# A mixture-of-experts tail in 140 units: row buffers for 32 units, landings reported five units late, a longer table of needs, blank units without weight loads

## The chip, the cores and the metric

The kernel runs on one NeuronCore of a Trainium2 chip. The time is the device time of one execution in microseconds (us). The kernel before took 716.58 us, the median of three runs (715.09 to 717.36). The engines are TensorE (PE, matmuls), VectorE (DVE), ScalarE (ACT), GpSimd (POOL, which issues the indirect DMAs here) and SyncE (SP, which issues nearly all other DMAs). Each runs its own list of instructions in order; they meet at semaphores. A DMA adds 16 to a semaphore when its data has landed.

## The reference

```
x = x + gnn(layernorm(x))          # 128 x 128 x 128 floats: 16384 tokens of 128
xf = layernorm(x).reshape(-1, 128)
top_w, top_i = top_k(xf @ Wg + bg, 2);  top_w = softmax(top_w)
for e in range(8):                 # H = 512
    h = gelu(xf @ W1[e] + b1[e])
    out = out + w_dense[:, e:e+1] * (h @ W2[e] + b2[e])
x = x + out
```

The biases bg of this input are uneven, so that the experts get very different numbers of tokens: of the lower-numbered of a token's two experts 2866, 2285, 657, 3756, 328, 6492, 0, 0 tokens fall on experts 0 to 7, and of the higher-numbered one 0, 33, 6, 172, 8, 297, 15868, 0. (These are counts of the reference's own choices for this input.)

## The kernel before

**Two stages.** The first takes the tokens in 16 chunks: the graph layer, the second layernorm, the two experts of each token, and its place in a list sorted by expert. POOL scatters the rows (260 floats: the normalised token, the running sum, weights, and where to go next) into `rows` in HBM, expert by expert. The second stage takes sorted rows in **units** of 256 rows of one expert. There are two passes, the first over the lower-numbered experts of all tokens, the second over the higher-numbered ones, with 70 units each (`NU`), so units 0 to 69 and 70 to 139. The first 32 units (`NE`) are full units that can start before all chunks are counted.

**What a unit does.** SP loads its 256 rows (`rows_in`, line 504, 260 KB), its expert's biases (`biases_in`, 532), and, only if the expert differs from that of three units before, each layer's weights (`layer_in`, 520, 512 KB a layer, into one of three slots). PE transposes the rows (1606), does layer 1 (1620 to 1622, 12 matmuls), layer 2 of the unit before (1633, 1634, 1638, 12 matmuls), and turns back the outputs of the unit two before (1649). ACT applies gelu, and DVE splits the values into high and low parts (1420, 1426). `sum_up` on DVE (1435, 1440) adds the expert's output to the rows of the unit three before; it stands ahead of the split of the current unit. POOL then scatters the 256 rows with two indirect DMAs (`scatter`): to their place for the second pass (line 691), or in the second pass to the output (688).

**SP's order.** At step k SP issues: layer 1's weights and the biases of unit k+2, layer 2's weights of unit k+1, then the rows of unit k+6. Each waits in that one list: weights for a free slot (the matmuls of three units before), rows for two things. One is the **buffer**: rows live in a ring of 16 buffers (`GR`), so that unit t waits until the scatter of unit t-16 has landed; units 0 to 31 use `first_rows`, space left by the first stage, and units from 32 on use `got`, so that units 32 to 47 find theirs free. The other is for units of the second pass the **need**: the number of first-pass units whose scattered rows must have landed. It is looked up in a table on the chip for the first 12 of them (`EARLY`); the 13th waits for all. The table is read into SP's registers by `entries` (line 486), 16 steps at a time.

**Reports.** POOL counts landings for SP in `s_landed` (line 674): before it hands over the scatter of unit t, its list waits until unit t-3 has landed, adds one, then waits for `sum_up` of unit t. The semaphore starts at 1.

**The experts here.** From the counts above and the code follow, before and after alike: units 0 to 31 hold experts 0, 1, 2, 3 and 5; units 32 to 37 expert 0, 38 to 41 expert 1, 42 and 43 expert 2, 44 to 49 expert 3, 50 and 51 expert 4, 52 to 66 expert 5, 67 to 69 are blank (nothing to do, same weights). In the second pass 70 and 71 are blank, 72 to 75 hold experts 1, 2, 3, 4, 76 and 77 expert 5, 78 to 139 expert 6. Weights are loaded in the kernel before for units 38 to 40, 42 to 46, 50 to 54 and 70 to 80 (among others). Unit 78 and all after it need 67 landed units, 0 to 66.

Of the kernel before, what the change touches and what calls it, by code (L numbers as in the profile page):

```python
# [8 lines left out]
I32 = mybir.dt.int32  # L9
U32 = mybir.dt.uint32  # L10
ALU = mybir.AluOpType
# [3 lines left out]
P = 128  # L15
# [70 lines left out]
def program(nc, x, x_turned, adj, edges, gate_weights, gate_biases, Wg, bg, W1, W2, biases, out):  # L86
# [15 lines left out]

    EARLY = 3 * GR // 4

# [6 lines left out]
    FULL = CHUNKS - 6  # L111
    NE = 2 * GR

    RING = 5
# [7 lines left out]

    ALL = 48 * (UNITS // 48 + 1)

    def unit(k):
# [15 lines left out]
    with ExitStack() as ctx:  # L141
        def sb(name, shape, dt=F32):
            return ctx.enter_context(nc.sbuf_tensor(name, list(shape), dt))

        def sem(name):
            return ctx.enter_context(nc.semaphore(name))
# [116 lines left out]
        got = row[:, 1:5].rearrange("p r (s j) k -> p (r s) j k", j=BLK)  # L263
        got_i = got.bitcast(I32)

# [8 lines left out]
        def rows_of_unit(t):  # L274
            return first_rows[t.slot(GR)] if t.index < NE else got[:, t.slot(GR)]
        to_row = sb("to_row", [P, GR, BLK], I32)
        in_hi = sb("in_hi", [P, IN, TILE], F32R)
# [122 lines left out]
        s_done = sem("unit_summed")  # L400
        s_out = [sem(f"unit_rows_scattered{i}") for i in range(GR)]

# [6 lines left out]
        def _(sp):  # L409
# [88 lines left out]
            def rows_in(t, both):  # L498
                if t.real:
                    at = sp.snap(both >> 4, min_val=0, max_val=BLANK + 1)  # L500
                    g = t.slot(GR)
                    if not NE <= t.index < NE + GR:
                        wait_slot(sp, s_out, 16 * BLK, t, 0)
                    sp.dma_start(rows_of_unit(t).rearrange("p j k -> p (j k)"),
                                 rows[bass.ds(at, TILE)].rearrange("(p j) k -> p (j k)", j=BLK)).then_inc(s_got[g], 16)
# [79 lines left out]
            for first in range(NE, UNITS, UT):  # L585
# [5 lines left out]
                for k in range(first, min(first + UT, UNITS)):  # L591
# [6 lines left out]
                    if k + AHEAD < UNITS:  # L598
                        wait_landed(k + AHEAD, needs)
                        rows_in(unit(k + AHEAD), early[k + AHEAD - NU] if 0 <= k + AHEAD - NU < AHEAD else now[i])  # L600
            for i in range(GR):
                sp.wait_ge(s_out[i], 16 * BLK * ((UNITS + GR - 1 - i) // GR))

        @block.gpsimd
        def _(pool):
# [66 lines left out]
            def landed(t):  # L672
                wait_slot(pool, s_out, 16 * BLK, t, 16 * BLK)
                pool.sem_inc(s_landed, 1)

            def scatter(t):
                second = t.index >= NU
                if 0 <= t.index - 3 < NU:
                    landed(t.back(3))
                wait_turn(pool, s_done, 1, t, 1)  # L680
                g = t.slot(GR)
                for j in range(BLK):
                    if t.index < NE:
                        at = bass.IndirectOffsetOnAxis(ap=rows_of_unit(t).bitcast(I32)[:, j, NEXT_AT:NEXT_AT + 1], axis=0)
                    else:
                        at = bass.IndirectOffsetOnAxis(ap=to_row[:, g, j:j + 1], axis=0)
                    if second:
                        pool.indirect_dma_start(out=out_rows, out_offset=at, in_=got[:, g, j, P:2 * P], in_offset=None,  # L688
                                                bounds_check=TOKENS - 1, oob_is_err=False).then_inc(s_out[g], 16)
                    else:  # L690
                        pool.indirect_dma_start(out=rows, out_offset=at, in_=rows_of_unit(t)[:, j, :], in_offset=None,  # L691
                                                bounds_check=NROWS - 1, oob_is_err=False).then_inc(s_out[g], 16)
# [179 lines left out]
        def _(dve):  # L872
# [7 lines left out]
            dve.memset(node_least[:, 0:2], 0.0).then_inc(s_iota, 1)  # L880
            dve.tensor_scalar(node_least[:, 2:3], node_i[:], -float(WR), 0.0, ALU.add, ALU.min).then_inc(s_iota, 1)
            dve.tensor_copy(slot_f[:], slot_i[:]).then_inc(s_iota, 1)
# [407 lines left out]
            def units_begun():  # L1290
# [11 lines left out]

                own(dve.tensor_tensor(change[:], expert[:, 2], expert[:, 0], ALU.not_equal))
                own(dve.tensor_reduce(first, at_unit[:, 0], AX_X, ALU.add))
# [123 lines left out]
            def sum_up(t):  # L1428
                g, second = t.slot(GR), int(t.index >= NU)
                held = rows_of_unit(t)  # L1430
                at = TOKEN_AT if second else NEXT_AT

                if t.index >= NE:
                    i = t.index if second else t.index - NE
                    dve.scalar_tensor_tensor(out=to_row[:, g, :], in0=skip[:, i, :], scalar=BIG, in1=got_i[:, g, :, at],
                                             op0=ALU.mult, op1=ALU.max)
                wait_turn(dve, s_o, 1, t, 1)
                for j in range(BLK):
                    w = held[:, j, W_AT + second:W_AT + second + 1]
                    last = dve.scalar_tensor_tensor(out=held[:, j, P:2 * P], in0=ps_o(t)[:, j, :], scalar=w,  # L1440
                                                    in1=held[:, j, P:2 * P], op0=ALU.mult, op1=ALU.add)
                last.then_inc(s_done, 1)
# [277 lines left out]
```

## Time and profile before

| what | value |
|---|---|
| median of three runs | 716.58 us (715.09 to 717.36) |
| the profiled execution | 716.63 us, its span 714.9 us |
| PE, ACT, DVE, POOL busy | 91%, 83%, 81%, 70% of the span |
| second stage | from about 214 us to the end |

The span is the time from the first to the last instruction of the profiled execution; 1.7 us lie around it. A profile view "waits" says who waited for whom; a timeline row is an instruction with its start, its length and, in brackets, the idle time of its engine before it and what ended it. Busy times of PE overlap within a stream, so stalls are read best from starts.

### The profile page before, as it was taken

To read this page: it belongs to the slowest core of one execution; us is meant where nothing else is said; L and a number is where in the kernel's file an instruction comes from. 1 tells how busy PE (TensorE), PEld (TensorE's weight loads), DVE (VectorE), ACT (ScalarE), POOL (GpSimd) and SP (SyncE) were. 2 spreads that over 40 slices of the span, in tenths; PEclk is the share of its full clock that TensorE was granted. 3 is DMA by queue.
4 is the path that set the end of the run, shared out by engine and by line. 5 is a ranking of instruction groups with operands and counts; after the bars stand their busy time and mean duration, and the time that the engine had idled before them with its cause. 6 is when DMAs were issued, how large, how long until landed. Compare 5 with 4: busy or idle time off the path is not lost.

```text
span 714.9 us, 18241 instructions
## 1 busy us (share of the span) xinstructions
PE 647.8 (91%) x4879; PEld 589.7 (82%) x4879; DVE 578.9 (81%) x2041; ACT 596.1 (83%) x1613; POOL 498.2 (70%) x471
## 2 busy tenths in 40 slices
PE   5979898998849999999998999998999999999991
PEld 4546665666539999899997999988999999999991
DVE  5899999999987889987876778776778787878781
ACT  4789999999968978788886878876888888888881
POOL 2643767666765677788777778777677777677774
PEclk9999999899979999999999999999999999999997
DMA  8999995548246897959999985689754444444211
GB/s 288 360 369 268 355 344 177 183 163 325 97 151 187 287 343 237 318 165 301 330 372 322 367 254 171 178 329 359 233 153 126 124 127 122 129 121 129 73 42 34
DMA packets 85500, 161.09 MB, mean 225 GB/s; under 512 B 32631, under 2 KB 36736, under 8 KB 85392
## 3 DMA queue, kind: packets, MB, share of 16 engines
q1 hardware_dynamic: 66032, 112.96, 50.4%
q0 software_dynamic: 18496, 46.70, 17.8%
q8 instruction: 41, 0.67, 0.4%
q14 instruction: 67, 0.55, 0.2%
q10 hardware_dynamic: 864, 0.21, 0.1%
HBM read 104.95 MB, written 57.23 MB: 227 GB/s over the span
## 4 chain that ended last, share of the span: by engine, by line
PE 31%; ACT 23%; POOL 14%; issue 12%; DVE 9%; DMA 7%; SPq 2%; POOLq 0%; DVEq 0%; ACTq 0%
POOL out_dram L688 8%; POOL rows L691 6%; ACT hs L750 5%; ACT row L759 5%; DMA rows<-row,to_row 4%; PE bank L1633 4%; PE bank L1638 4%; PE bank L1620 4%; PE bank L1634 4%; ACT t_loop L741 4%; PE bank L1621 4%; PE bank L1622 4%; ACT t_in L734 3%; PE bank L1606 2%; PE bank L1649 2%
## 5 line engine op out<-in xcount | busy, mean ns | idle before, releaser
L846 ACT ACTIVATE act_f<-bank,b_t 128x256 f32<-128x256 f32 x560 | 219.4, 476 | 23.3 <-PE bank L1622 13.0
L688 POOL DMA_INDIRECT out_dram<-row,to_row x140 | 164.0, 1171 | 60.9 <-issue 55.4
L1426 DVE TENSOR_TENSOR act_lo<-act_f,act_hi 128x1024 fp32r<-128x1024 f32 x140 | 172.0, 1229 | 12.1 <-ACT act_hi L850 0.2
L646 POOL DMA_INDIRECT rows<-row,slot_low x128 | 134.8, 1053 | 64.7 <-issue 34.1
L1420 DVE CAST act_hi<-act_f 128x512 fp32r<-128x512 f32 x140 | 61.5, 439 | 90.5 <-ACT act_f L846 90.4
L1620 PE MATMUL bank<-in_hi,w_t 128*128 128x256 f32 x376 | 113.8, 303 | 7.0 <-DMA w_t<-w_split 5.9
L691 POOL DMA_INDIRECT rows<-row,to_row x76 | 93.3, 1228 | 25.0 <-issue 20.9
L1622 PE MATMUL bank<-in_hi,w_t 128*128 128x256 f32 x376 | 105.7, 281 | 0.0
L1621 PE MATMUL bank<-in_lo,w_t 128*128 128x256 f32 x376 | 105.7, 281 | 0.0
L836 ACT ACTIVATE in_hi<-bank 128x256 fp32r<-128x256 f32 x140 | 53.9, 385 | 58.0 <-PE bank L1606 57.4
L1633 PE MATMUL bank<-act_hi,w_t 128*128 128x256 f32 x376 | 100.4, 301 | 0.0
L1634 PE MATMUL bank<-act_hi,w_t 128*128 128x256 f32 x376 | 92.2, 280 | 0.0
L850 ACT ACTIVATE act_hi<-act_f 128x512 fp32r<-128x512 f32 x140 | 90.8, 649 | 0.0
L1620 PEld LDWEIGHTS bank<-in_hi,w_t 128*128 128x128 f32 x376 | 71.4, 190 | 8.9 <-DMA w_t<-w_split 7.5
L1621 PEld LDWEIGHTS bank<-in_lo,w_t 128*128 128x128 f32 x376 | 71.6, 190 | 0.0
L1622 PEld LDWEIGHTS bank<-in_hi,w_t 128*128 128x128 f32 x376 | 71.2, 189 | 0.0
L1634 PEld LDWEIGHTS bank<-act_hi,w_t 128*128 128x128 f32 x376 | 70.9, 189 | 0.0
L1633 PEld LDWEIGHTS bank<-act_hi,w_t 128*128 128x128 f32 x376 | 70.8, 188 | 0.1
L856 ACT ACTIVATE y_t<-bank,b_t 128x256 f32<-128x256 f32 x140 | 65.6, 469 | 2.4 <-PE bank L1638 2.4
L1440 DVE SCALAR_TENSOR_TENSOR row<-bank,row 128x128 f32<-128x128 f32 x216 | 65.2, 344 | 1.6 <-PE bank L1649 1.6
L750 ACT ACTIVATE hs<-xs,shift,rstd 128x128 f32<-128x128 f32 x128 | 53.5, 645 | 8.6 <-DVE t_sum L990 6.6
L1414 DVE TENSOR_TENSOR in_lo<-bank,in_hi 128x256 fp32r<-128x256 f32 x140 | 58.1, 415 | 2.6 <-ACT in_hi L836 2.6
(278 smaller groups left out, 1787.6 us busy)
## 6 DMA issues: line engine op xcount, KB each, us to landing
row<-rows SPq DMA_DIRECT2D x108, 260.0 KB, 3.1
w_t<-w_split SPq DMA_DIRECT2D x52, 512.0 KB
w_up<-w_split SPq DMA_DIRECT2D x28, 512.0 KB
xs<-in_x_dram SPq DMA_DIRECT2D x16, 512.0 KB, 5.3
x_t<-in_x_turned_dram SPq DMA_DIRECT2D x16, 512.0 KB, 6.4
rows<-ends_rep SPq DMA_DIRECT2D x15, 260.0 KB, 7.7
xs<-rows SPq DMA_DIRECT2D x10, 260.0 KB
b_t<-in_biases_dram SPq DMA_DIRECT2D x140, 2.5 KB
```

The source lines that it names most:

```text
L646: pool.indirect_dma_start(out=rows, out_offset=bass.IndirectOffsetOnAxis(ap=slot_low[:, r, b:b + 1], axis=0), in_=row[:, r, b, :], in_offs ...
L688: pool.indirect_dma_start(out=out_rows, out_offset=at, in_=got[:, g, j, P:2 * P], in_offset=None, bounds_check=TOKENS - 1, oob_is_err=Fals ...
L691: pool.indirect_dma_start(out=rows, out_offset=at, in_=rows_of_unit(t)[:, j, :], in_offset=None, bounds_check=NROWS - 1, oob_is_err=False) ...
L750: last = act.activation(hs[:, t.slot(2), b, :], xs[:, t.slot(4), b, :], ACT.Identity, scale=rstd[:, 0, b:b + 1], bias=shift[:, 0, b:b + 1])
L846: last = act.activation(act_f[:, s, c, :], ps_h(t, half)[:, i, :], ACT.Gelu, bias=b_t[:, w, c:c + 1])
L850: act.activation(act_hi[:, t.slot(LATE + 1), 0:FC // 2], act_f[:, s, 0:FC // 2], ACT.Copy).then_inc(s_half, 1)
L1426: dve.tensor_tensor(act_lo[:, s], act_f[:, t.slot(2)], act_hi[:, s].bitcast(F32), ALU.subtract).then_inc(s_hlo, 1)
L1620: pe.matmul(dst, hi, in_hi[:, s], start=True, stop=False)
L1621: pe.matmul(dst, hi, in_lo[:, s], start=False, stop=False)
L1622: last = pe.matmul(dst, lo, in_hi[:, s], start=False, stop=True)
L1633: pe.matmul(ps_y(t), hi, act_hi[:, s, c, :], start=(c == 0), stop=False)
L1634: pe.matmul(ps_y(t), lo, act_hi[:, s, c, :], start=False, stop=False)
```

## The change

Four things. The ring gets 32 buffers (`LANES`): from unit 32 on a unit uses first the 16 of `got`, then the 16 of `first_rows`, and so on, and waits for the scatter of its buffer's last user (`lane`, `uses`); units 16 to 31 wait as before. POOL reports unit t-5, not t-3, before the scatter of unit t. Needs are looked up for 24 units. In the second pass a blank unit counts as one whose expert has not changed, so that it loads no weights, and the three units behind the blank ones do (here 70 and 71 load nothing; 72 to 80 load as before).

```diff
-    EARLY = 3 * GR // 4
+    EARLY = 24
...
+    LANES = 2 * GR
...
+    def lane(k):
+
+        return k % GR if k < NE else (GR + k - NE) % LANES
+
+    def uses(k):
+
+        return sum(lane(i) == lane(k) for i in range(k))
...
         def rows_of_unit(t):
-            return first_rows[t.slot(GR)] if t.index < NE else got[:, t.slot(GR)]
-        to_row = sb("to_row", [P, GR, BLK], I32)
+            i = lane(t.index)
+            return first_rows[i] if i < GR else got[:, i - GR]
+        to_row = sb("to_row", [P, LANES, BLK], I32)
...
-                    if not NE <= t.index < NE + GR:
-                        wait_slot(sp, s_out, 16 * BLK, t, 0)
+                    if uses(t.index):
+                        sp.wait_ge(s_out[lane(t.index)], 16 * BLK * uses(t.index))
...
             def landed(t):
-                wait_slot(pool, s_out, 16 * BLK, t, 16 * BLK)
+                pool.wait_ge(s_out[lane(t.index)], 16 * BLK * (uses(t.index) + 1))
                 pool.sem_inc(s_landed, 1)
 
             def scatter(t):
                 second = t.index >= NU
-                if 0 <= t.index - 3 < NU:
-                    landed(t.back(3))
+                if 0 <= t.index - 5 < NU:
+                    landed(t.back(5))
                 wait_turn(pool, s_done, 1, t, 1)
...
-            dve.tensor_scalar(node_least[:, 2:3], node_i[:], -float(WR), 0.0, ALU.add, ALU.min).then_inc(s_iota, 1)
+            dve.memset(node_least[:, 2:3], -float(WR)).then_inc(s_iota, 1)
...
-                own(dve.tensor_tensor(change[:], expert[:, 2], expert[:, 0], ALU.not_equal))
+                own(dve.tensor_tensor(change[:, 0:1], expert[:, 2, 0:1], expert[:, 0, 0:1], ALU.not_equal))
+                own(dve.scalar_tensor_tensor(out=change[:, 1:2], in0=expert[:, 2, 1:2], scalar=expert[:, 0, 1:2], in1=is_unit[:],
+                                             op0=ALU.not_equal, op1=ALU.mult))
```

SP's list at step 42, at the rows of unit 48, before: `unit_rows_scattered0` counts the scatters from buffer 0, here that of unit 32; the DMA behind it loads unit 48.

```order
L522 UNCONDITIONAL_BRANCH [waits second_layer_of_slot2]
L504 ISA [waits unit_rows_scattered0]
L504 DMA row<-rows 128x520
L513 REGISTER_ALU
L514 REGISTER_ALU
L514 COMPARE_AND_BRANCH
L520 ISA [waits hidden_in_psum]
L520 DMA w_t<-w_split 128x1024
```

And after, where the names say that unit 48 waits for the scatter of unit 16 from that buffer:

```order
L531 UNCONDITIONAL_BRANCH [waits second_layer_of_slot1]
L513 ISA [waits unit_rows_scattered0]
L513 DMA w_in<-rows 128x520
L522 REGISTER_ALU
L523 REGISTER_ALU
L523 COMPARE_AND_BRANCH
L529 ISA [waits hidden_in_psum]
L529 DMA w_t<-w_split 128x1024
```

The list is the same; unit 48's rows go into `w_in`, the first buffer of `first_rows`, and the semaphore is that of a scatter 32 units back, not 16.

POOL's list at the turn of the passes, before, from unit 69's scatter. `unit_rows_scattered2` is the landing of unit 66, `unit_summed` the sums of the unit about to be scattered:

```order
L691 DMA rows<-row,to_row 229888x260 [waits unit_rows_scattered2,unit_summed]
L691 DMA rows<-row,to_row 229888x260
L688 DMA out_dram<-row,to_row 16384x128 [waits unit_rows_scattered3,unit_summed]
L688 DMA out_dram<-row,to_row 16384x128
L688 DMA out_dram<-row,to_row 16384x128 [waits unit_rows_scattered4,unit_summed]
L688 DMA out_dram<-row,to_row 16384x128
```

And after, from unit 69 too; `unit_rows_scattered16` is the landing of unit 64, `unit_rows_scattered18` that of unit 66:

```order
L700 DMA rows<-row,to_row 229888x260 [waits unit_rows_scattered16,unit_summed]
L700 DMA rows<-row,to_row 229888x260
L697 DMA out_dram<-row,to_row 16384x128 [waits unit_rows_scattered17,unit_summed]
L697 DMA out_dram<-row,to_row 16384x128
L697 DMA out_dram<-row,to_row 16384x128 [waits unit_rows_scattered18,unit_summed]
L697 DMA out_dram<-row,to_row 16384x128
```

The landing of unit 66, which SP needs before it may load unit 78, is waited for ahead of unit 69's scatter before, and ahead of unit 71's after: four scatter instructions later in POOL's list.

## Rows read from the trace of the kernel before

**Rows 1.** Windows: us, busy (x) of PE, PEld, DVE, ACT, POOL; clock, DMA, GB/s.

```profile
350.00:400.00 50.00, 46.37 (x392) 45.42 (x391) 35.98 (x85) 39.48 (x98) 38.78 (x33) 1.00 0.97 339
...
450.00:500.00 50.00, 45.91 (x383) 44.51 (x382) 35.27 (x81) 38.62 (x96) 37.70 (x33) 1.00 0.86 296
...
550.00:600.00 50.00, 50.00 (x432) 50.00 (x432) 39.49 (x93) 43.71 (x109) 36.93 (x31) 1.00 0.45 123
```

**Rows 2.** PE's timeline, its idle times near 380 and 480 us.

```profile
380.32 0.38 PE L1633 MATMUL bank<-act_hi,w_up 128*128 128x256 f32 x1 [1.13 <-DMA w_up<-w_split]
...
383.41 0.39 PE L1620 MATMUL bank<-in_hi,w_t 128*128 128x256 f32 x1 [1.21 <-DMA w_t<-w_split]
...
485.02 0.39 PE L1620 MATMUL bank<-in_hi,w_t 128*128 128x256 f32 x1 [2.83 <-DMA w_t<-w_split]
```

**Rows 3.** Waits of SP in 364:388 and in 466:482: us, times, longest.

```profile
SPq L504 <- DMA rows<-row,to_row: 8.9, 4, 5.7
...
SPq L504 <- POOLq L674: 7.1, 1, 7.1
```

**Rows 4.** SP's timeline: its DMAs around the two waits.

```profile
366.40 0.33 SPq L520 DMA_DIRECT2D w_t<-w_split  x1
...
373.45 0.33 SPq L520 DMA_DIRECT2D w_t<-w_split  x1
...
471.28 0.33 SPq L520 DMA_DIRECT2D w_t<-w_split  x1
479.24 0.33 SPq L504 DMA_DIRECT2D row<-rows  x1
479.98 0.33 SPq L520 DMA_DIRECT2D w_t<-w_split  x1
```

**Rows 5.** The same windows view, around the two waits.

```profile
360.00:372.00 12.00, 12.00 (x106) 12.00 (x105) 9.38 (x24) 10.71 (x27) 9.79 (x8) 1.00 1.04 404
372.00:376.00 4.00, 3.78 (x33) 3.52 (x31) 2.75 (x8) 2.97 (x8) 3.09 (x4) 1.00 0.79 253
376.00:384.00 8.00, 4.59 (x35) 3.89 (x34) 4.70 (x11) 3.59 (x9) 5.45 (x6) 1.00 1.02 362
...
468.00:476.00 8.00, 7.25 (x63) 7.02 (x61) 6.63 (x17) 6.15 (x16) 6.25 (x5) 1.00 1.04 406
476.00:480.00 4.00, 3.80 (x33) 3.56 (x32) 2.31 (x7) 3.07 (x8) 3.09 (x4) 1.00 0.49 180
```

**Rows 6.** POOL's timeline: scatters with idle time, and those about the passes' turn.

```profile
383.34 0.97 POOL L691 DMA_INDIRECT rows<-row,to_row  x1 [1.07 <-DVE row L1440]
...
471.64 1.14 POOL L691 DMA_INDIRECT rows<-row,to_row  x1 [0.84 <-DMA rows<-row,to_row]
473.09 0.97 POOL L691 DMA_INDIRECT rows<-row,to_row  x1 [0.31 <-issue]
...
478.90 1.41 POOL L691 DMA_INDIRECT rows<-row,to_row  x1 [0.30 <-issue]
...
483.17 0.97 POOL L688 DMA_INDIRECT out_dram<-row,to_row  x1 [0.30 <-issue]
```

**Rows 7.** DVE's timeline of the same stretch.

```profile
475.18 0.60 DVE L1440 SCALAR_TENSOR_TENSOR row<-bank,row 128x128 f32<-128x128 f32 x2
...
479.45 0.60 DVE L1440 SCALAR_TENSOR_TENSOR row<-bank,row 128x128 f32<-128x128 f32 x2
```

**Rows 8.** POOL's reports (line 674) in 478:480 and in 275:279; POOL's timeline behind.

```profile
L674 POOLq EVENT_SEMAPHORE  x1: 17/17/17, 479.0 to 479.0; - x1
...
L674 POOLq EVENT_SEMAPHORE  x3: 17/17/17, 276.0 to 278.4; - x3
...
288.82 1.50 POOL L691 DMA_INDIRECT rows<-hs  x1 [0.30 <-issue]
```

**Rows 9.** Line 691 in 430:450, its DMAs from issue to landing.

```profile
DMA to landing us min/median/max: 3.1/3.2/3.2
```

**Rows 10.** Loads of the table into SP's registers, all steps after the first.

```profile
L486 SPq TENSOR_LOAD <-unit_table x12: 504/1240/3881, 316.4 to 645.5; - x12
```

More of the change, by code:

```diff
@@ L263, in program @@
         got = row[:, 1:5].rearrange("p r (s j) k -> p (r s) j k", j=BLK)
-        got_i = got.bitcast(I32)
         first_rows = []
@@ L400, in program @@
         s_done = sem("unit_summed")
-        s_out = [sem(f"unit_rows_scattered{i}") for i in range(GR)]
+        s_out = [sem(f"unit_rows_scattered{i}") for i in range(LANES)]
         s_landed = sem("first_pass_units_landed")
@@ L600, in _ @@
                         rows_in(unit(k + AHEAD), early[k + AHEAD - NU] if 0 <= k + AHEAD - NU < AHEAD else now[i])
-            for i in range(GR):
-                sp.wait_ge(s_out[i], 16 * BLK * ((UNITS + GR - 1 - i) // GR))
+            for k in range(UNITS - LANES, UNITS):
+                sp.wait_ge(s_out[lane(k)], 16 * BLK * (uses(k) + 1))
         @block.gpsimd
@@ L677, in scatter @@
                 second = t.index >= NU
-                if 0 <= t.index - 3 < NU:
-                    landed(t.back(3))
+                if 0 <= t.index - 5 < NU:
+                    landed(t.back(5))
                 wait_turn(pool, s_done, 1, t, 1)
-                g = t.slot(GR)
+                g = lane(t.index)
                 for j in range(BLK):
@@ L687, in scatter @@
                     if second:
-                        pool.indirect_dma_start(out=out_rows, out_offset=at, in_=got[:, g, j, P:2 * P], in_offset=None,
+                        pool.indirect_dma_start(out=out_rows, out_offset=at, in_=rows_of_unit(t)[:, j, P:2 * P], in_offset=None,
                                                 bounds_check=TOKENS - 1, oob_is_err=False).then_inc(s_out[g], 16)
@@ L1428, in sum_up @@
             def sum_up(t):
-                g, second = t.slot(GR), int(t.index >= NU)
+                g, second = lane(t.index), int(t.index >= NU)
                 held = rows_of_unit(t)
@@ L1434, in sum_up @@
                     i = t.index if second else t.index - NE
-                    dve.scalar_tensor_tensor(out=to_row[:, g, :], in0=skip[:, i, :], scalar=BIG, in1=got_i[:, g, :, at],
+                    dve.scalar_tensor_tensor(out=to_row[:, g, :], in0=skip[:, i, :], scalar=BIG, in1=held.bitcast(I32)[:, :, at],
                                              op0=ALU.mult, op1=ALU.max)
```

## The prediction

> **What bounds the kernel now.** I read the windows first. PE carries the second stage: where nothing disturbs it, it runs 432 matmuls in 50 us [rows 1], and with 28 matmuls and turns in a unit that is 15.4 units, 3.24 us each (3.26 between starts of undisturbed units in the timeline). The same 50 us hold 392 of them at 350 to 400 us and 383 at 450 to 500 us [rows 1]: 40 and 49 missing, 4.6 and 5.7 us of stall. Only such stalls can be won; ACT, DVE and POOL are less busy than PE [rows 1] and set no pace by themselves.
>
> PE's timeline says what ended the stalls: weights that had not landed, at 380.32 for unit 45's second layer, at 383.41 for unit 46 and at 485.02 for unit 75 [rows 2]. Then I ask why the weights were late. Ahead of each stands a wait of SP at line 504, the rows' load: 5.7 us at the longest for a scatter to land, and 7.1 us for one report of POOL [rows 3]. SP's timeline shows both as holes: nothing between 366.40 and about 372.7, where the rows of unit 48 wait for buffer 0 (unit 32's scatter), and the first-layer weights of unit 45, next in the list, leave at 373.45; and nothing between 471.28 and 479.24, where the rows of unit 78 wait until units 0 to 66 are reported, and the weights of unit 75 leave at 479.98 [rows 4]. They reach PE 5.04 us later.
>
> So the second hole hangs on POOL. The first scatter to the output (483.17) is unit 70's; two scatters a unit back, those at 471.64 and 473.09 are unit 66's [rows 6]. It ended at 474.06 and was reported at 479.0 [rows 8], 4.9 us of landing. Unit 70's sums were ready at 475.78 (DVE's row at 475.18) [rows 7], yet it was scattered at 483.17: POOL is 7 us behind and works without a rest. Its time is set by its own list, not by PE.
>
> **The change, part by part.** *32 buffers.* The rows of unit 48 now wait for unit 16's scatter, long landed. The first hole goes, and unit 45's weights leave at about 367.6, not 373.45 (366.40, and the 1.2 us that SP's own list took). But the DMA engines were full then (share 1.04, 404 GB/s), so that what comes back is not 5.9 us. Bounds: from below, what they left unused, 0.21 of 4 us at 372 to 376 and the 10% by which 362 GB/s lies under 404 during the next 8 us [rows 5], 1.6 us; I go down to 1.0. From above, the whole stall, 4.6 us. I take 2.5 us, since the two later loads queue behind as before. Call it G: PE runs units 47 to 72 G earlier. At units 50 to 54 weights are late by their own mass; nothing there changes.
>
> *What G is worth at the end: nothing by itself.* Unit 75 cannot begin before the report of unit 66 plus SP's list (0.98 us from 479.0 to 479.98) plus the load (5.04 us). G makes PE wait longer there. The two stalls must not be added.
>
> *Reports five units late.* This adds a wait of another kind: before the report of unit 66 POOL must have handed over unit 70's scatter, which needs unit 70's sums, ready at 475.78 less G, about 473.3 [rows 7]. That lies ahead of the landing, so it costs nothing while POOL is behind. Nor does the length of the queue: at 278.4 POOL had reported unit 9, that is, handed over unit 11's scatter, which ran only at 288.82 [rows 8]; ten microseconds, with eight instructions between. Six are needed here. So the report comes with the landing, as before.
>
> What is taken away is a rest of POOL. Its sequencer waited for landings; six times between 310 and 484 us the engine stood longer than its usual 0.30 us between scatters, from 0.38 to 1.07 us (the two longest in [rows 6]), 3.85 us in all and 2.05 us over the usual. That goes.
>
> Against it stands a catch. A scatter instruction takes 0.97 us, but one that is open while DVE's sums run ends 0.26 us behind them: the one of 478.90 took 1.41 us and ended at 480.31, DVE's row of 479.45 at 480.05 [rows 6, 7]. The extra is up to 0.7 us and comes once for each unit of PE. With PE's stall at 380 shorter by G, POOL meets one more of these: up to 0.8 us back; but a shift may also let one slip by, another 0.7 us. Unit 66's scatter then ends 2.05 less 0.8 earlier, or up to 2.7: between 471.3 and 472.8. I take 472.3, 1.8 us earlier.
>
> *Blank units without weights.* Four loads of 512 KB fewer, at 456 to 464 us. Units 72 to 80 load as before. The queue was full at 468 to 476 (1.04, 406 GB/s) [rows 5], and 2 MB at that rate are 5 us of it. PE no longer stalls at units 73 and 74, which changes nothing for unit 75. But the landing of unit 66 shares the engines with less. From above it takes the 4.9 us of before; from below 2.2 us, for around 440 us a landing came 3.2 us after the issue [rows 9], of which the instruction's own 0.97 us is to be taken off. With weights of 72 to 74 still in flight I take 4.2 us. Report at 476.5, against 479.0: 2.5 us. Bounds: 471.3 + 2.2 = 473.5 and 472.8 + 4.9 = 477.7, a gain of 5.5 to 1.3 us.
>
> From there SP's list runs as before, one DMA after the other, and paces PE to unit 80 by it. The loads start with emptier engines; I give 0.5 us for that, none at the low end. Sum: 3.0 us.
>
> [...]
>
> *Needs for 24 units.* Unit 82 no longer asks for all units, which would be reported later now; this only keeps a new wait away. But the table is read once more at step 80, with 24 entries. Such a read takes 0.5 to 3.9 us [rows 10], and behind it stand the biases of unit 82 and the rows of unit 86. Both have some 3 us and more to spare. I count 0, bounds 0 and 1. *DVE's extra small instruction* in unit 19's step: under 0.2 us, counted as nothing.
>
> The profiled execution took 716.63 us, its span 714.9 and 1.7 around it; the median is 716.58. So the forecast is 716.6 - 3.0 = **713.6 us**.
>
> **The rivals.** *POOL gains nothing (0.26).* The rests it loses are eaten by DVE's sums, since POOL stays in step with them at one unit in 3.26 us; landing as slow as before. The report then comes at 478 to 479, the gain is 0 to 2 us: 714.6 to 716.6. For it speaks that in undisturbed stretches POOL's period equals PE's; against it, that each of the six rests lies where it was out of step.
>
> *The report comes in time (0.06).* Were unit 66 reported before SP asks (about 469 us), all stalls of units 73 to 80 but the DMA's own would go: G plus some 4.5 us, 709.5 us. It needs POOL 7 us earlier; nothing in the rows gives that.
>
> *Five units late is too late (0.08), slower.* If POOL's sequencer cannot run that far ahead here, the report of unit 66 comes when unit 70's scatter is begun: at 483.2 less 1.8 us, 481.4 at the earliest, or at 484.5 with its second instruction [rows 6]. Unit 75 then starts 2.4 to 5.5 us later than before, 719 to 722 us. It decides from the point where the report lies more than 0.5 us behind 479.0, which the emptier engines give back. Against it: the ten microseconds of [rows 8].
>
> *The buffers do not do what they say*, because something else holds SP at 367 us: then G is 0, and by the above the end hardly changes. It is inside the first case.
>
> **How the numbers follow.** The forecast has 0.60. Its own bounds are a gain of 1.3 to 6.0 us, 710.6 to 715.3. Adding the upper part of "nothing" and leaving out the fast and the slow rival gives a range of 711.0 to 717.0, where the lowest 0.4 us are left out as the meeting of two ends. The kernel's runs can tell about 0.3%, 2.15 us, from no change. Faster by more: 0.85 of the forecast's 0.60, the fast rival's 0.06 and a little of the second, 0.58. Within: 0.33. Slower by more: the slow rival, 0.09.
>
> **What would show it.** SP has no wait for a scatter in 364 to 388, and unit 46 starts at about 381, not 383.41. POOL's scatters there never stand over 0.31 us. One wait of SP for line 674's counterpart remains near 469 to 477, longer than 7.1 us; the report ends it at 476.5, and the first output scatter starts at about 481. PE's last long idle, before unit 75, is about 5 us, longer than 2.83, with the start at 482 rather than 485.02. 76 weight loads, not 80. If the report comes at or after 479, the prediction is wrong in POOL's part; if PE does not idle before unit 75, in what binds.

## The result, and the profile after

The changed kernel is slower: 718.48 us, the median of 17 runs (715.68 to 720.71), against 716.56 us for the kernel before in 17 runs of the same session (713.34 to 719.03). The ratio is 1.003 with a 95% interval of 1.0017 to 1.0042. The prediction said 713.6 us, in a range of 711.0 to 717.0, and faster. It was wrong by 4.9 us.

The profiled execution of the changed kernel took 715.68 us (span 713.9), 1 us less than that of before. It is the lowest of the changed kernel's times, so the traces tell where time goes in one execution, and the medians tell what the change is worth.

Windows of the changed kernel, same columns as [rows 1] and [rows 5]:

```profile
350.00:400.00 50.00, 48.97 (x415) 48.26 (x414) 38.64 (x89) 41.67 (x104) 39.95 (x34) 1.00 1.01 364
450.00:500.00 50.00, 46.83 (x376) 46.46 (x375) 34.49 (x80) 37.84 (x94) 38.63 (x32) 0.93 0.76 265
550.00:600.00 50.00, 50.00 (x429) 50.00 (x428) 39.40 (x95) 43.34 (x109) 36.81 (x31) 1.00 0.44 120
```

The first row is what the buffers were for: 415 matmuls instead of 392 [rows 1]. The second is worse than before, 376 instead of 383, and its granted clock is 0.93, not 1.00. The third is the one that matters most: in a stretch with no stall in either kernel, where the change touches nothing that PE waits for, there are 429 matmuls instead of 432. Between the starts of units 90 and 135 a unit takes 3.281 us, against 3.256.

SP's waits of 364 to 388 and of 466 to 482 us, the counterpart of [rows 3], and its DMAs behind the second [rows 4]:

```profile
SPq L534 <- SPq L534: 1.7, 2, 1.0
SPq L529 <- PE bank L1649: 1.6, 2, 1.3
SPq L529 <- PE bank L1633: 0.4, 1, 0.4
```

```profile
SPq L513 <- POOLq L683: 6.8, 1, 6.8
```

```profile
467.55 0.47 SPq L529 DMA_DIRECT2D w_t<-w_split  x1
475.31 0.33 SPq L513 DMA_DIRECT2D row<-rows  x1
476.06 0.33 SPq L529 DMA_DIRECT2D w_t<-w_split  x1
```

No wait for a scatter is left in the first stretch; the wait for the report of unit 66 is, nearly as long as before. The weights of unit 75 leave at 476.06, not 479.98. POOL's scatters of units 66 and 67, and the reports of units 66 and 67 (line 683 is line 674 of before):

```profile
467.61 1.70 POOL L700 DMA_INDIRECT rows<-row,to_row  x1 [0.30 <-DMA rows<-row,to_row]
469.61 0.97 POOL L700 DMA_INDIRECT rows<-row,to_row  x1 [0.30 <-issue]
470.89 1.70 POOL L700 DMA_INDIRECT rows<-row,to_row  x1 [0.30 <-issue]
```

```profile
L683 POOLq EVENT_SEMAPHORE  x2: 17/17/17, 475.1 to 476.7; - x2
```

The first output scatter began at 480.70 (before: 483.17, [rows 6]). Last, PE's idle times, near 380 us and before unit 75, and the windows of the time around it:

```profile
378.32 0.38 PE L1631 MATMUL bank<-in_hi,w_t 128*128 128x256 f32 x1 [0.94 <-DMA w_t<-w_split]
...
480.46 0.58 PE L1631 MATMUL bank<-in_hi,w_t 128*128 128x256 f32 x1 [3.17 <-DMA w_t<-w_split]
```

```profile
476.00:480.00 4.00, 1.29 (x12) 1.06 (x10) 2.57 (x6) 1.69 (x5) 3.24 (x3) 0.96 0.79 240
480.00:484.00 4.00, 3.54 (x16) 3.54 (x17) 0.00 (x0) 1.42 (x4) 3.08 (x4) 0.50 0.98 307
484.00:488.00 4.00, 4.00 (x26) 4.00 (x25) 2.67 (x6) 1.96 (x6) 3.09 (x4) 0.68 1.05 385
```

Behind PE's idle time of 3.17 us the granted clock is 0.50, the lower of its two levels (1.2 instead of 2.4 GHz): the matmul of 480.46 takes 0.58 us, not 0.38. So unit 75, which began 4.6 us earlier than before, was followed by unit 76 only 5.99 us later. The trace thus offered two suspects: **CLOCK**, the low clock that a longer idle time may bring, and **PACE**, the 0.025 us more in every unit; and **CHANCE**, that both belong to one execution.

### The profile page after: what moved, and what is told of

Its sections match the earlier page's. It is cut to its first block and busy times, and to the rows that moved or that the text cites. A ratio compares the mean times of both kernels' runs of the same rounds, so it can differ in the third digit from the quotient of the medians.

```text
span 713.9 us, 18263 instructions
## 1 busy us (share of the span) xinstructions
PE 649.7 (91%) x4879; PEld 594.4 (83%) x4879; DVE 579.8 (81%) x2042; ACT 596.3 (84%) x1613; POOL 500.2 (70%) x471
## 5 line engine op out<-in xcount | busy, mean ns | idle before, releaser
L697 POOL DMA_INDIRECT out_dram<-row,to_row x76 | 88.3, 1161 | 32.1 <-issue 29.9
L700 POOL DMA_INDIRECT rows<-row,to_row x44 | 55.2, 1255 | 13.4 <-issue 11.6
L1649 PE MATMUL bank<-act_lo,w_t 128*128 128x256 f32 x376 | 59.8, 281 | 0.0
```

The lines of the kernel that those rows point to most:

```text
L697: pool.indirect_dma_start(out=out_rows, out_offset=at, in_=rows_of_unit(t)[:, j, P:2 * P], in_offset=None, bounds_check=TOKENS - 1, oob_is ...
L1649: last = pe.matmul(ps_y(t), hi, act_lo[:, s, c, :], start=False, stop=(c == FC - 1))
```

## The experiments

First one table for the points that I read in each trace, since the first stage ends anywhere from 212.2 to 215.8 us and shifts all that follows. It has the starts of units 75, 81 and 139, counted from the start of unit 0 in the same trace; the mean distance of unit starts from 90 to 135; PE's matmuls in 550 to 600 us; and the measured ratio to the kernel before, where there were enough runs for one.

| kernel | 75 | 81 | 139 | us a unit | matmuls | ratio (95%) |
|---|---|---|---|---|---|---|
| before | 270.9 | 292.2 | 480.7 | 3.256 | 432 | |
| before_again | 268.5 | 290.2 | 478.7 | 3.256 | 432 | 1.0003 (0.9980 to 1.0025) |
| changed | 267.5 | 290.1 | 480.0 | 3.281 | 429 | 1.0030 (1.0017 to 1.0042) |
| after_again | 267.7 | 290.9 | 480.8 | 3.281 | 429 | 1.0025 (1.0006 to 1.0044) |
| only_buffers | 270.0 | 292.1 | 481.9 | 3.281 | 429 | 1.0039 (1.0020 to 1.0058) |
| only_reports | 271.0 | 293.9 | 482.4 | 3.256 | 433 | 1.0013 (0.9994 to 1.0032) |
| only_blank | 269.5 | 290.7 | 479.1 | 3.256 | 433 | 0.9982 (0.9962 to 1.0002) |
| moved_128 | 268.8 | 292.8 | 482.3 | 3.275 | 430 | 1.0033 (1.0015 to 1.0050) |
| as_before | 267.6 | 290.6 | 479.1 | 3.257 | 433 | 0.9990 (0.9975 to 1.0006) |
| as_before_three_late | 268.4 | 290.6 | 479.1 | 3.257 | 432 | 0.9991 (0.9972 to 1.0011) |
| rows_later | 264.4 | 288.0 | 476.7 | 3.257 | 432 | 0.9933 (0.9910 to 0.9957) |
| rows_later_16 | 264.4 | 286.4 | 476.6 | 3.256 | 433 | 0.9933 (0.9909 to 0.9957) |
| before_rows_later | 269.0 | 289.1 | 477.6 | 3.256 | 432 | 0.9957 (0.9935 to 0.9978) |

The same kernel differs from itself by 2 us in the first three columns (before and before_again), so only larger differences count there. The pace of a unit repeats to 0.001 us.

### The parts of the change, one by one

after_again is the changed kernel once more.

> The changed kernel again, for a second trace. In its first trace the 26 us before unit 75 run as forecast (unit 75 starts at 480.46 us, not 485.02), but it comes behind one idle time of PE of 3.2 us, then the granted clock is at its lower level for some 7 us, and undisturbed units take 3.28 us, not 3.26. Theory CLOCK: the idle time before unit 75 brings the low clock each time, at 480 to 487 us. Theory PACE: something in the changed kernel makes every unit 0.025 us longer, so that 432 matmuls in 50 us are again 429 here. Theory CHANCE: both are of that one execution; this trace has full clock there or 3.26 us a unit. The time is 718 to 719 us by CLOCK and PACE (ratio 1.003).

The pace is there again, 429 matmuls; the low clock is not. Around and behind unit 75's start the second trace has

```profile
480.00:488.00 8.00, 6.01 (x48) 5.78 (x49) 2.91 (x7) 4.18 (x11) 6.03 (x7) 1.00 0.96 336
488.00:496.00 8.00, 7.77 (x65) 7.37 (x64) 5.83 (x13) 6.43 (x16) 6.22 (x6) 1.00 1.05 379
```

CLOCK falls as the cause: with full clock here, unit 139 begins no earlier (480.8 us after unit 0, 480.0 in the first trace). The medians over all runs say the same. Each run lists its mean granted clock; the median of it is 0.967 for the changed kernel and 0.966 for as_before (below), which has a clock as low and takes 0.4% less. PACE stands. only_buffers, only_reports and only_blank take one part each; the first is the changed kernel with this undone:

```diff
-    EARLY = 24
+    EARLY = 3 * GR // 4
...
-                if 0 <= t.index - 5 < NU:
-                    landed(t.back(5))
+                if 0 <= t.index - 3 < NU:
+                    landed(t.back(3))
```

and with the two edits for blank units undone.

> The kernel before with the 32 buffers alone. By my prediction the first stall shrinks by 2.5 us and the second grows by as much, so 0 to 1 us is won: ratio 0.999 to 1.000. CLOCK: the idle time before unit 75 is then longer than in the kernel before (over 5 us with the weights of 70 and 71 still loaded), the clock falls behind it, and the kernel is 2 to 4 us slower, ratio 1.003 to 1.006. PACE, if the buffers are what makes units longer (the rows stand at other addresses): 429 matmuls in 50 us, 2 to 3 us slower, with the full clock at 480 us.

Slower by 0.39%, with the pace of 3.281 us. By the clock alone it could not be told, since that was low here too (0.97 in 450 to 500 us); by the pace it can: the 32 buffers carry it.

only_reports is the kernel before with `t.back(5)` and `t.index - 5`, nothing else.

> The kernel before with reports five units late alone. By my prediction POOL loses its rests and the report of unit 66 comes 0 to 2 us earlier; the first stall stays, so that the idle time before unit 75 is 1 to 2.8 us and the clock stays: ratio 0.997 to 1.000. CLOCK: no low clock here, since the idle time is no longer than before. PACE, if it is the reports: 429 matmuls in 50 us in the second pass cannot be, since no report is given there; the ratio stays at or under 1.000. If reports five late are themselves harmful, the report of unit 66 comes behind 479 us and the ratio is over 1.002.

1.0013, no difference that these runs can tell; the pace is that of before, 3.256 us. A report of unit 66 that comes sooner is not seen: SP waited 6.7 us for it, and unit 75 began 271.0 us after unit 0. POOL did come earlier: it ended the scatter of unit 66 257.6 us after unit 0, against 259.9 and 258.4 in the two traces of before. But the report came only 8.2 us behind that, where before has 4.9 and 4.6. The reports of units 60 and 63 to 65 came 6.1 us behind their scatters, each 1.1 us behind the sums of the unit four later, which POOL's list now has to pass first; unit 66's came 3.2 us behind the sums of unit 70, of which 2.1 us stay unexplained. So here reporting five units late took back what it gave. The second scatter of unit 66, the last row of unit 70's sums, and the report of unit 66:

```profile
471.43 0.97 POOL L691 DMA_INDIRECT rows<-row,to_row  x1 [0.30 <-issue]
```

```profile
476.78 0.60 DVE L1440 SCALAR_TENSOR_TENSOR row<-bank,row 128x128 f32<-128x128 f32 x2
```

```profile
L674 POOLq EVENT_SEMAPHORE  x1: 17/17/17, 480.6 to 480.6; - x1
```

The clock was low here too (0.97), behind an idle time of 3.0 us. only_blank is the kernel before with the two edits on DVE.

> The kernel before where units 70 and 71 load no weights, alone. The stalls before units 73 and 74 (1.0 and 0.5 us) go and that before unit 75 grows by the same, from 2.83 to some 4.3 us, since the report of unit 66 comes at most 0.7 us earlier. By my prediction: 0 to 1 us won, ratio 0.999 to 1.000. CLOCK: one idle time of over 3 us before unit 75, so the clock falls for some 7 us and the kernel is 2 to 3 us slower, ratio 1.003 to 1.004. PACE: 432 matmuls in 50 us, as in the kernel before.

0.9982, 1.3 us less, by an interval that just includes no change; 0 to 1 us was expected. The idle time before unit 75 was 3.3 us, longer than the changed kernel's 3.17, and the clock stayed at 1.00. So an idle time of that length does not always bring the low clock.

### What makes a unit longer

With 32 buffers `to_row` is twice as long, 256 bytes a partition instead of 128. All tiles declared behind it move up by 128: `in_hi` and `in_lo`, `act_f`, `act_hi`, `act_lo`, `y_t`. PE's matmuls of both layers read `in_hi`, `in_lo`, `act_hi` and `act_lo`, and its turns back read `y_t`. moved_128 is the kernel before with that alone, as_before the changed kernel without it. before_again ran beside them.

```diff
         to_row = sb("to_row", [P, GR, BLK], I32)
+        unused = sb("unused", [P, GR, BLK], I32)
```

```diff
-        to_row = sb("to_row", [P, LANES, BLK], I32)
+        unused = sb("unused", [P, GR, BLK], I32)
...
         y_t = sb("y_t", [P, BACK, TILE])
+        to_row = sb("to_row", [P, LANES, BLK], I32)
```

> The kernel before as an experiment of its own: a second trace of it, and the scale for small differences. Ratio 1.000, within its interval. ADDRESSES and every other theory of the unit's pace: 432 or 433 matmuls in 50 us at 550 to 600 us. If it shows 429, the pace is of the execution and not of the kernel, and the pace theory falls. If it shows a low clock near 485 us, the low clock is not brought by the change.

> The kernel before with one unused tile of 128 bytes a partition behind to_row, and nothing else: in_hi, in_lo, act_f, act_hi, act_lo and y_t move up by 128 bytes, as they do in the changed kernel, whose to_row is twice as long. The three kernels with 32 buffers ran 429 or 430 matmuls in 50 us in undisturbed stretches, the three without them 432 or 433. Theory ADDRESSES: PE's matmuls are slower by 1 to 3 ns each with these tiles there; 429 here, and over some 110 units of 0.025 us the kernel is 2.5 us slower, ratio 1.003 to 1.004. Theory BUFFERS: the longer ring itself (more semaphores, other tiles for the rows) makes the pace; then 432 here and ratio 1.000.

> The changed kernel with to_row behind all other tiles and 128 unused bytes in its old place, so that in_hi to y_t stand where they stood in the kernel before. ADDRESSES: 432 matmuls in 50 us, and the gain that I forecast appears in part: 2.5 us less than the changed kernel, ratio to before 0.998 to 1.000, and 0.996 if nothing else fails. BUFFERS: 429, ratio 1.003, as the changed kernel.

The windows of 550 to 600 us in before_again, moved_128 and as_before, one row each:

```profile
550.00:600.00 50.00, 50.00 (x432) 50.00 (x431) 39.81 (x95) 43.67 (x110) 37.33 (x31) 1.00 0.45 120
```

```profile
550.00:600.00 50.00, 50.00 (x430) 50.00 (x429) 38.92 (x92) 43.48 (x108) 36.81 (x31) 1.00 0.47 129
```

```profile
550.00:600.00 50.00, 50.00 (x433) 50.00 (x432) 39.62 (x95) 43.72 (x109) 36.57 (x31) 1.00 0.45 122
```

An unused tile of 128 bytes makes the kernel before 0.33% slower, 2.4 us; taking the shift away from the changed kernel brings it from 1.0030 to 0.9990, 2.9 us. That is the pace: 0.019 to 0.025 us in each of the 110 or so units that run undisturbed, 2.1 to 2.8 us. ADDRESSES holds, BUFFERS falls. (The changed kernel's 3.281 us against moved_128's 3.275 is left unexplained.) The loss is spread over the matmuls of both layers, 0 to 2 ns each. The groups of line 1622 in the kernel before and of its counterpart 1623 in moved_128, from 520 to 680 us (columns as in the page: busy us, mean ns):

```profile
L1622 PE MATMUL bank<-in_hi,w_t 128*128 128x256 f32 x131 | 36.6, 280 | 0.0
```

```profile
L1623 PE MATMUL bank<-in_hi,w_t 128*128 128x256 f32 x132 | 37.2, 282 | 0.0
```

before_again also shows the low clock in the kernel before, so that it does not take the change to bring it:

```profile
480.00:488.00 8.00, 5.96 (x38) 5.87 (x38) 4.41 (x10) 3.69 (x9) 6.17 (x7) 0.79 0.97 343
```

as_before_three_late is as_before with `t.back(3)` again.

> The same kernel as as_before, but landings are reported three units late again. By my prediction POOL then keeps its rests and the report of unit 66 comes up to 2 us later than with five: 0.000 to 0.003 above as_before. Rival: with the buffers and the blank part the report comes as early, and three late is as good or better, since alone the later reports measured 1.0013: 0.000 to 0.003 below as_before.

0.9991 and 0.9990: five or three units late is no difference that can be measured.

### Which places are bad

Six more shifts, each read from one trace. The places are worked out from the kernel's list of tiles, each begun at a multiple of 32 bytes. No trace shows an address: what the runs show are the effects of shifts, and if the first tile begins elsewhere than I took it, every place below, also that of the weights, is off by the same amount. The first five have an unused tile of 64, 192, 256, 320 or 512 bytes in the place of moved_128's; act_moved_64 has one of 64 bytes between `in_lo` and `act_f`.

> As moved_128, with 64 unused bytes instead of 128: in_hi, act_hi and the others then begin at a multiple of 512 bytes. Units at 3.256 us (432 matmuls in 50 us) stand at 448 past such a multiple, units at 3.275 us (430) at 64 past. ADDRESSES, if it is the place within 512 bytes that counts and 0 is the best: 3.25 us or less. If it is the neighbourhood to other tiles: somewhere between 3.256 and 3.275.

> 192 unused bytes behind to_row: in_hi to y_t begin 128 past a multiple of 256. Seen so far: 0 past it 3.304 us a unit, 64 past it 3.275, 192 past it 3.256 (three times). If the cost falls with the place within 256 bytes: 3.26 or less. If 0 and 128 are alike: 3.30.

> 256 unused bytes: the tiles begin 192 past a multiple of 512. If the cost grows with the distance moved it is over 3.275 us a unit; if it hangs on the place within 512 bytes or within 256, it is one of the two values seen, 3.256 or 3.275.

> 320 unused bytes: in_hi to y_t begin 256 past a multiple of 512, that is 0 past one of 256. If the place within 256 bytes counts, 3.304 us a unit as with 64 unused bytes; if that within 512, not.

> 512 unused bytes: the tiles stand 448 past a multiple of 512 as in the kernel before, but 512 bytes higher. If the place within 512 bytes counts, 3.256 us a unit; if the neighbourhood or the absolute place, not.

> 64 unused bytes between in_lo and act_f: act_f, act_hi, act_lo and y_t begin at a multiple of 512, in_hi and in_lo stay at 448 past one. moved_64, where all moved, was at 3.304 us a unit, the kernel before at 3.256. Layer 2's operands alone (two of 24 kinds of matmuls move act_lo, a third act_hi): half of the 0.048 us, 3.28; if it is in_hi and in_lo alone, 3.256; if it is act alone, 3.304.

| place of the tiles past a multiple of 256 bytes | kernels | us a unit | matmuls in 550 to 600 |
|---|---|---|---|
| 192 | before (two traces), moved_256, moved_512 | 3.256 | 432 |
| 64 | moved_128 | 3.275 | 430 |
| 128 | moved_192 | 3.278 | 429 |
| 0 | moved_64, moved_320 | 3.304 | 426 |
| `in_` 192, `act_` 0 | act_moved_64 | 3.281 | 429 |

The place within 256 bytes sets the pace, and not the distance moved: moved_320 equals moved_64, moved_256 and moved_512 equal before. Both layers take part, since moving the operands of layer 2 (with `y_t`) costs 0.025 of 0.048 us. (Of the 24 matmuls of the two layers 8 move `act_hi` and 4 `act_lo`, not as I wrote ahead of that run.) I had expected a multiple of 512 bytes to be the best place; it is the worst of those tried. moved_192 fits neither of its two forecasts. The slowest, moved_64, in the same window:

```profile
550.00:600.00 50.00, 50.00 (x426) 50.00 (x425) 38.88 (x91) 43.06 (x107) 37.31 (x31) 1.00 0.45 127
```

The last of this kind moves the weights instead (and `w_in` and the biases, which stand with them), from 160 past a multiple of 256 to 192, with `in_hi` to `y_t` 256 bytes higher, that is, at their good place of 192. It is built on rows_later (below).

```diff
+        unused_w = sb("unused_w", [P, 8], I32)
         w_in = sb("w_in", [P, 2, 2, H])
...
-        unused = sb("unused", [P, GR, BLK], I32)
+        unused = sb("unused", [P, 88], I32)
```

> rows_later with w_in, w_up, w1_t and w2_t 32 bytes higher (192 past a multiple of 256 instead of 160) and in_hi to y_t 256 bytes higher (192 past one, as in the kernel before). If only the place of the operands that PE moves counts, 432 matmuls in 50 us and the ratio of rows_later, 0.993. If the place of the weights counts as much, 3.24 to 3.28 us a unit and 0.988 to 0.998.

426 matmuls, 3.303 us a unit, and a ratio of 1.0021 where rows_later has 0.9933: 32 bytes under the weights cost 6 us, more than either forecast. So the place of the weights counts too. Whether it is their distance that counts (32 is good; 0 and 96 within 256 bad; 160 and 224 between) or two places, each by itself, these runs don't tell.

### What holds PE at units 73 to 80

as_before has the pace of before and an earlier report, and still gains only 0.1%. rows_later is as_before with SP's order changed: from unit 76 on rows are issued four units ahead, not six, and so behind the weights of units 75 and 76.

```diff
-            needs = None
+            needs, later = None, NU + 6
+            row_at = {}
...
-                    if k + AHEAD < UNITS:
-                        wait_landed(k + AHEAD, needs)
-                        rows_in(unit(k + AHEAD), early[k + AHEAD - NU] if 0 <= k + AHEAD - NU < AHEAD else now[i])
+                    row_at[k + AHEAD] = early[k + AHEAD - NU] if 0 <= k + AHEAD - NU < AHEAD else now[i]
+                    u = k + AHEAD if k + AHEAD < later else k + AHEAD - 2
+                    if u < UNITS and (u < later) == (k + AHEAD < later):
+                        wait_landed(u, needs)
+                        rows_in(unit(u), row_at[u])
```

> The kernel as_before (the changed kernel with in_hi to y_t at their old places), and SP issues the rows of units 76 to 139 four units ahead instead of six, so that the rows of unit 78, which wait for the report of unit 66, stand two steps later in SP's list, behind the weights of units 75 and 76. Theory RELEASE (my prediction's): the report of unit 66 sets when unit 75 begins, 67.5 us after unit 48's stretch and 267.6 us after unit 0, because the weights of 75 stand behind it. Then SP meets the wait only about when the report comes, its wait falls from some 7 to under 2 us, unit 75 starts 3 to 4 us earlier and the kernel takes 3 to 4 us less: ratio 0.994 to 0.995 to before. Rival MASS: the DMA engines are the bound from unit 72 to 80 (nine loads of 1 MB, with rows and scatters); then the stall before unit 75 is only spread over units 73 to 80, unit 81 starts as in as_before (290.6 us after unit 0), and the ratio is 0.999.

0.9933, 4.8 us faster than before; in its trace unit 75 begins 264.4 us after unit 0, 3.2 us earlier than in as_before, and unit 81 2.6 us earlier. RELEASE holds: the loss lay in what stands behind the wait. SP's wait for the report in as_before and in rows_later, and what then ended PE's idle times of 470 to 490 us in each:

```profile
SPq L514 <- POOLq L684: 6.3, 1, 6.3
```

```profile
480.19 0.38 PE L1632 MATMUL bank<-in_hi,w_t 128*128 128x256 f32 x1 [3.07 <-DMA w_t<-w_split]
```

```profile
SPq L514 <- POOLq L687: 4.1, 1, 4.1
```

```profile
474.72 0.44 PE L1621 MATMUL bank<-ident,row 128*128 128x128 f32 x2 [0.81 <-DMA row<-rows]
478.53 0.44 PE L1621 MATMUL bank<-ident,row 128*128 128x128 f32 x2 [0.35 <-DMA row<-rows]
483.34 0.44 PE L1621 MATMUL bank<-ident,row 128*128 128x128 f32 x2 [1.33 <-DMA row<-rows]
```

The wait is 4.1 us, not under 2 as I wrote: the report came 264.5 us after unit 0, in as_before 262.2. In rows_later_16, below, it came at 262.0, and SP waited 0.9 us. And three short idle times for rows stand where one of 3 us for weights stood. MASS has its share: from unit 75 to 81 rows_later takes 23.6 us where six units need 19.5.

before_rows_later and rows_later_16 ask what the change's parts add to that. The first has none of them, the second all but the buffers (and the addresses of before).

> The kernel before (16 buffers, reports three late, unit 70 and 71 with weights, its addresses) with the rows of units 76 to 139 four units ahead instead of six. rows_later, which has the parts of the change too, was at 0.9933. RELEASE alone: nearly all of it comes from SP's order, ratio 0.993 to 0.995. If the change's parts carry it (an earlier report, four loads fewer, the free buffers): 0.996 to 0.999.

> rows_later without the 32 buffers: 16 buffers and the addresses of before, but reports five late, needs for 24 units, no weights for units 70 and 71, and the rows of units 76 to 139 four units ahead. If the buffers' free rows are worth something (the stall at units 44 to 47 and 52 to 55), the ratio lies 0.001 to 0.003 above rows_later's 0.9933; if the buffers are worth nothing, as only_buffers and as_before hint, 0.993 to 0.994; if none of the change's parts is worth anything, it is as before_rows_later, 0.9957.

SP's order alone brings 0.9957, between the two forecasts. With the reports five late, the longer table and the blank units without weights it is 0.9933, and the buffers add nothing to that (0.9933 with them). The two intervals overlap, so the difference of 0.0024 is likely, not shown. rows_later and rows_later_16 both beat the kernel before and the changed one by more than their intervals.

## Why the prediction was wrong, point by point

**What bounds the kernel: right.** The prediction said that unit 75 hangs on the report of unit 66 through SP's list. rows_later only put that wait behind two units' weights, and it gained 0.6% on as_before. Two of the signs named did not come: SP's wait was 6.8 us, not longer than 7.1, and PE's idle time before unit 75 was 3.17 us, not about 5. By the prediction's own terms it should have said 3.8: the 2.83 us of before, plus 2.5 (G), plus 1.5 (the stalls before units 73 and 74), less 3.0.

**The first stall and G: sign right, too large.** SP had no wait for a scatter in 364 to 388, and unit 46 began at 381.9 us, forecast about 381. But G was sized from one execution. In before_again the same 50 us hold 410 matmuls, not 392 [rows 1]:

```profile
350.00:400.00 50.00, 48.95 (x410) 47.60 (x409) 37.90 (x88) 41.18 (x103) 37.37 (x35) 1.00 1.00 357
```

and as_before, with 32 buffers, has 405. The stall of 4.6 us was a bad case. It cost the forecast nothing, since G was said not to reach the end, which only_buffers bears out: its unit 75 begins 270.0 us after unit 0, between the 270.9 and 268.5 of before's two traces.

**The report of unit 66: right in time.** Forecast 476.5 us, measured 475.1, and 1.2 us of the difference is that unit 0 started at 213.0 and not at 214.2. But before's trace was one of the later ones, see below. The scatter of unit 66 ended at 469.61 + 0.97 = 470.6, forecast 472.3. But it was not taken apart rightly: five units late against three makes no difference (as_before, as_before_three_late). POOL's rests went. Over units 15 to 45 it took 2.9 to 3.0 us a unit and caught up, but from unit 50 on 3.28 us, 1.70 + 0.30 + 0.97 + 0.30 in the rows above, which is PE's pace. From there on it is as the rival *POOL gains nothing* said. The rival *too late* did not come here, where the report came with the landing, 4.5 us behind the scatter; in only_reports it came in part.

**The load of unit 75's weights:** issued at 476.06, used at 480.46, 4.40 us; 5.04 was taken from before, less 0.5 for emptier engines. The Trainium skill ("DMA: Bandwidth & Descriptors", "Anatomy of one DMA") has a fit for DMAs that POOL issues, 2.0 us plus the bytes over 436 GB/s. For the rows and the weights here, 790 KB, that would be an estimate of 3.8 us, below both measured times; but SP issues these two, so that the fit need not hold for them.

**Blank units: not contradicted.** 76 weight loads as forecast, and alone 0.9982 (0.9962 to 1.0002). Between 468 and 476 us the engines' share fell from 1.04 to 0.58:

```profile
468.00:476.00 8.00, 8.00 (x71) 8.00 (x70) 6.53 (x17) 7.11 (x19) 6.62 (x5) 1.00 0.58 213
```

**From the release to unit 80: the first step that failed.** The prediction said that from the report on "SP's list runs as before, one DMA after the other, and paces PE to unit 80", so that 3.0 us at unit 75 would be 3.0 us at the end. as_before, which has before's pace of a unit, shows what became of them. Four traces have before's schedule and its pace: before, before_again, moved_256 and moved_512. Times are counted from unit 0:

| | report of unit 66 | unit 75 | unit 81 | from 75 to 81 |
|---|---|---|---|---|
| the four, each | 264.9, 263.0, 263.8, 266.5 | 270.9, 268.5, 269.8, 271.9 | 292.2, 290.2, 291.5, 294.2 | 21.4, 21.6, 21.7, 22.4 |
| their mean | 264.5 | 270.3 | 292.0 | 21.8 |
| as_before, as_before_three_late | 262.2, 263.1 | 267.6, 268.4 | 290.6, 290.6 | 23.0, 22.3 |

So, on average, the report came 1.9 us earlier, not 2.5, unit 75 2.3 us, not 3.0, and unit 81 1.4 us: about 0.9 us were paid back in between. The medians have 0.7 us (as_before gains 0.1%, and by its interval at most 0.25%). The four traces lie 3.4 us apart at unit 75, so these steps are best values, not measured ones; that the 3.0 us did not arrive is measured.

Why some were paid back is argued and not shown. The DMA engines are full behind the release in before, before_again and as_before alike (share 1.03 to 1.05 in 488 to 496, as in the rows of after_again above), and a released list doesn't make them faster: SP issued unit 80's first-layer weights 8.4 us before unit 80 began in as_before, 7.5 in before. I had read the fullness of the queue ahead of the wait [rows 5] and not asked for it behind. rows_later, which reached unit 75 3.2 us earlier than as_before, kept 2.6 of them at unit 81, so that such a payback is in any case partial.

**What the prediction did not have: the second and larger step.** The sentence on the buffers counted waits, and nothing for the tile that grew. 128 bytes cost 2.4 to 2.9 us, measured both ways. This alone turns the 0.7 us of as_before into a loss of 2. In numbers: forecast −3.0; not reached at unit 75 or paid back behind it, +2.3; addresses, +2.9; sum +2.2, measured 0.0030 × 716.6 = +2.1. (The +2.3 is what as_before lacks to 3.0, so the sum had to come out.) The prediction's part on what would show it named no row for the pace of undisturbed units, the first one that should be compared. Nothing in the trace of before could have given the size of the shift's price, but the shift was to be read from the diff, and a loss from it belonged into the range. The rival on the buffers stopped at a G of zero.

**Needs for 24 units, DVE's small instruction:** no cost is seen. The longer read took up to 3.9 us as before [rows 10]:

```profile
L495 SPq TENSOR_LOAD <-unit_table x13: 681/1589/3940, 315.6 to 643.5; - x13
```

## What to carry to other kernels

Compare first a stretch in which neither kernel stalls: three matmuls fewer in 50 us told more than all the waits, and they came from a tile that grew by 128 bytes in front of PE's operands. So a change that resizes a tile is measured together with the same change with all others kept at their places, and in a tuned kernel new tiles go behind the ones that the bottleneck reads.

A wait in an in-order list costs what stands behind it. Here it paid to put the waiting DMA two steps later (0.9957 alone, 3.1 us), and not to make what it waits for come earlier (as_before, 0.9990). And a stall read from one execution needs a second trace before it is worth a term: the 4.6 us near 380 us (40 matmuls missing of 432) were 2.5 us (22 missing) in the next one.

## What the runs showed of the hardware

- **The place of matmul operands in SBUF changes TensorE's pace.** Over the placements tried a unit of 28 matmuls took 3.256 to 3.304 us. For the values that PE moves, with the weights at 160 past a multiple of 256 bytes, 192 was best, 64 and 128 cost 0.02 us, 0 cost 0.048 us (1.5%; times the 110 or so undisturbed units an estimate of 5 us); moving the weights by 32 bytes cost 0.047 us. The pace repeated with a period of 256 bytes (moved_256, moved_512, moved_320). All places tried are multiples of 32 bytes. The Trainium skill, "SBUF — State Buffer", has in its section "Door 1: The DMA port swizzle" lines of 16 bytes, by which all of them would be alike, and says in "SBUF: two separate sides" that PE never waits on anyone there. No run here shows what PE waits for, only that the place of its own operands decides.
- **The low clock is not tied to one length of idle time.** It followed idle times of 3.17 us (changed), and 2.04 us in before_again, but not one of 3.3 us (only_blank) or 3.07 us (as_before). Here is before_again's:

```profile
482.13 0.38 PE L1620 MATMUL bank<-in_hi,w_t 128*128 128x256 f32 x1 [2.04 <-DMA w_t<-w_split]
```

It comes and goes with the execution in both kernels. It doesn't explain the medians: those of the mean granted clock are 0.967 (changed) and 0.966 (as_before), and as_before is 0.4% faster.
- **An indirect DMA of POOL that is open during a sum of DVE ends 0.25 us behind it.** In the trace of before, 101 of the 232 scatters between 320 and 690 us took longer than 1.02 us. 98 of them overlap a sum (line 1440), and 91 of these end 0.24 to 0.27 us behind it. Of the 131 of usual length, 0.97 us, only 9 overlap one. Once POOL had caught up to a fixed distance (from unit 50 in the changed kernel), POOL kept to the pace of DVE's sums with nothing to wait for: 3.28 us a unit, one of its two instructions 1.70 us long, the other 0.97. No run here shows what the instruction waits for.
